# Graph attention scores: destination terms from one matmul, spread by DMA, mask on GpSimd, source term on ScalarE

## What is computed

```python
h = jnp.einsum('blc,oc->blo', x, W).reshape(Bb, Ll, HEADS, HD).transpose(0, 2, 1, 3)   # x is layer-normed, 4 heads of 32
a_src = jnp.sum(h * att_src, axis=-1, keepdims=True)
a_dst = jnp.sum(h * att_dst, axis=-1, keepdims=True)
e = a_src + jnp.swapaxes(a_dst, 2, 3)          # e[i, j] = source score of i + destination score of j
e = jnp.where(e >= 0, e, NEG_SLOPE * e)
e = jnp.where(adj_mask[:, None, :, :], e, fill)
alpha = jax.nn.softmax(e, axis=-1)
out = jnp.einsum('bhij,bhjd->bhid', alpha, h)
```

## Time and profile before

| | |
|---|---|
| median of 3 runs | 1985.65 us (1980.44 to 1990.24) |
| the profiled execution | 1984.17 us, span 1982.4 us |
| PE busy | 1698.9 us, 86% |
| DVE busy | 1450.5 us, 73% |
| ACT busy | 926.4 us, 47% |
| POOL busy | 958.7 us, 48% |
| mean granted TensorE clock | 0.956 |

### The profile page before, as it was taken

One profiled execution on the slowest core, in us unless ns is written; L12 is line 12 of the kernel. 1 busy time (PEld: TensorE's weight loads), 2 busy tenths in 40 slices (PEclk: granted clock), 3 DMA queues, 4 the chain that ended last, 5 costly groups with the idle time before them and its releaser, 6 DMA issues.

```text
span 1982.4 us, 39651 instructions
## 1 busy us (share of the span) xinstructions
PE 1698.9 (86%) x10546; PEld 1308.2 (66%) x10546; DVE 1450.5 (73%) x5051; ACT 926.4 (47%) x2779; POOL 958.7 (48%) x852
## 2 busy tenths in 40 slices
PE   3667777999999999999999999999999999988675
PEld 2545566777777777777777777777777777766343
DVE  3556666878888788788887888888888888865532
ACT  1344433555555554555554555445555555543121
POOL 1143466554445555555544555545555444554433
PEclk9888888999999999999999999999999999988897
DMA  4000111222222212222222222122222222212221
GB/s 121 7 26 20 37 33 37 43 40 41 43 41 43 43 34 37 45 43 42 42 42 41 41 44 43 31 41 44 44 40 43 42 44 40 38 34 40 38 32 18
DMA packets 142416, 79.26 MB, mean 40 GB/s; under 512 B 33048, under 2 KB 137564, under 8 KB 141949
## 3 DMA queue, kind: packets, MB, share of 16 engines
q0 software_dynamic: 47232, 34.92, 12.2%
q1 hardware_dynamic: 94973, 41.80, 8.4%
...
## 4 chain that ended last, share of the span: by engine, by line
PE 54%; DVE 20%; issue 8%; POOL 4%; ACT 4%; DMA 1%; DVEq 0%; POOLq 0%; SPq 0%; ACTq 0%
PE bank L1056 7%; PE bank L1075 6%; PE bank L967 5%; PE bank L1060 5%; PE bank L893 5%; PE bank L1068 4%; PE bank L980 4%; PE bank L1002 3%; PE bank L1009 2%; DVE z L638 2%; PE bank L929 2%; DVE hg L858 2%; POOL routed L398 2%; DVE fx L660 2%; PE bank L1019 1%
## 5 line engine op out<-in xcount | busy, mean ns | idle before, releaser
L419 POOL DMA_INDIRECT out<-ys,xt x264 | 426.3, 1615 | 519.3 <-DMA out<-ys,xt 252.6
L398 POOL DMA_INDIRECT routed<-fx,slot x256 | 256.2, 1001 | 141.5 <-DVE slot L779 77.5
L503 ACT ACTIVATE p<-ub,nm 128x128 f32<-128x128 f32 x512 | 163.6, 390 | 277.4 <-DVE nm L712 277.4
L1075 PE MATMUL bank<-w_s,hsT 128*128 (+1 forms) x1584 | 232.1, 283 | 27.8 <-ACT hsT L545 20.4
L858 DVE SCALAR_TENSOR_TENSOR hg<-sg,bank 128x341 f32<-128x341 f32 x264 | 134.7, 510 | 163.2 <-ACT sg L538 161.8
L1075 PEld LDWEIGHTS bank<-w_s,hsT 128*128 128x128 f32 (+1 forms) x1584 | 205.2, 193 | 68.5 <-issue 61.4
L1056 PE MATMUL bank<-w_s,xT 128*128 x528 | 218.4, 496 | 19.6 <-DVE xT L852 7.7
L1060 PE MATMUL bank<-w_s,xT 128*128 x528 | 202.7, 466 | 4.0 <-DVE hu L866 0.4
L511 ACT ACTIVATE p<-bank,nm 128x128 f32<-128x128 f32 x512 | 145.5, 365 | 118.1 <-DVE nm L718 118.0
L544 ACT ACTIVATE hsT<-bank 128x256 f32<-128x256 f32 x264 | 101.1, 383 | 154.0 <-PE bank L1068 152.8
L1068 PE MATMUL bank<-ident,hu 128*128 128x128 f32 (+1 forms) x792 | 136.3, 282 | 33.1 <-DVE hu L866 15.7
...
## 6 DMA issues: line engine op xcount, KB each, us to landing
xt<-routed SPq DMA_DIRECT2D x264, 65.0 KB, 1.8
xs<-in_x SPq DMA_DIRECT2D x32, 256.0 KB, 3.1
out<-bs SPq DMA_DIRECT2D x32, 256.0 KB, 2.3
out<-ys,xt POOLq DMA_INDIRECT x264, 3.4
routed<-fx,slot POOLq DMA_INDIRECT x256
...
```

What stands on the lines that cost most here:

```text
L398: pool.indirect_dma_start(routed, bass.IndirectOffsetOnAxis(slot[p][:, i:i + 1], 0), fx[i // GB][p][:, i % GB, :], None).then_inc(S[f"sc{p ...
L419: pool.indirect_dma_start(out_rows, bass.IndirectOffsetOnAxis(xt[r][:, C:C + 1].bitcast(I32), 0), ys[r][:], None, compute_op=ALU.add).then ...
L503: last = act.activation(p1[j % 2][:, h, :], ub[j % 2][:, h, :], ACT.Exp, bias=nm1[:, j, h:h + 1])
L1075: last = pe.matmul(y_p[:, 0:C], hsT[r % 2][0:n, c, :], w2_s[0:n, bass.ds(e, 1), c, :].rearrange("p a c -> p (a c)"), start=c == 0, stop=c ...
```

## The change

The destination scores no longer come from `term1`. One matmul (`G.e`) of `wd`, now 128x128 with 4 filled columns, with all of xnT gives all destination scores of the group as 4 rows of 512 numbers. ACT copies them to `dT`. SP writes them to a DRAM buffer `dst_d` (`G.dw`, one DMA) and reads them back with 4 DMAs (`G.dr`), one for each batch, each of which puts the same 512 numbers on all 128 partitions of `dst`. POOL adds the mask in place (`G.m.j`), 512 wide. ACT adds the source score with 4 activations of 128 columns with a bias (`G.a.j`) and writes `ub`. DVE does leaky ReLU in place and the row maximum; its add from PSUM is gone. `mask` and `dst` are double buffered. The table `ORDER` is a new one: not only the new steps but most of the others stand in other places.

```diff
-            wd = sb("wd", [C, NH, L])
+            wd = sb("wd", [C, 128])
...
+                def put_dst():
+                    sp.wait_ge(S["dT"], g + 1)
...
+                    sp.dma_start(dst_d[p * GB:(p + 1) * GB, :].rearrange("b (h l) -> h b l", h=NH), dT[:]).then_inc(S["dd"], 16)
+
+                def get_dst():
+                    sp.wait_ge(S["dd"], 16 * (g + 1))
...
+                    for j in range(GB):
+                        row = dst_d[p * GB + j:p * GB + j + 1, :]
+                        sp.dma_start(dst[p][:, j, :], bass.AP(row.tensor, row.offset, [[0, L], [1, NH * L]])).then_inc(S[f"dq{j}"], 16)
...
+                def cut(j):
+                    pool.wait_ge(S[f"dq{j}"], 16 * (g + 1))
+                    if j == 0:
+                        pool.wait_ge(S["mask"], g + 1)
+                    d = dst[p][:, j, :].rearrange("p (h l) -> p h l", h=NH)
+                    pool.tensor_tensor(d, d, mask[p][:, j, :].unsqueeze(1).broadcast_to([L, NH, L]), ALU.add).then_inc(S["dm"], 1)
...
+                def e():
+                    act.wait_ge(S["dT_ps"], g + 1)
...
+                    act.activation(dT[:].rearrange("h b l -> h (b l)"), g0[0:NH, :], ACT.Copy).then_inc(S["dT"], 1)
+
+                def a_(j):
+                    act.wait_ge(S["dm"], 4 * g + j + 1)
+                    act.wait_ge(S["hE"], 2 * g + 1 + j // 2)
...
+                    for h in range(NH):
+                        o = h * GW + HD
+                        last = act.activation(ub[j % 2][:, h, :], dst[p][:, j, h * L:(h + 1) * L], ACT.Identity,
+                                              bias=hE[:, j, o:o + 1])
+                    last.then_inc(S["u"], 1)
...
                 def scores1(j):
-
-                    dve.wait_ge(S["P_ps"], 4 * g + j + 1)
...
-                    dve.tensor_tensor(tb[:], g0[:].rearrange("p (h l) -> p h l", h=NH),
-                                      hE[:, j, 0:NH * GW].rearrange("p (h w) -> p h w", w=GW)[:, :, HD:HD + 1].broadcast_to([L, NH, L]),
-                                      ALU.add).then_inc(S["t"], 1)
...
+                    dve.wait_ge(S["u"], 4 * g + j + 1)
+                    u = ub[j % 2]
+                    uf = u[:].rearrange("p h l -> p (h l)")
+                    dve.scalar_tensor_tensor(out=uf, in0=uf, scalar=0.2, in1=uf, op0=ALU.mult, op1=ALU.max).then_inc(S["t"], 1)
...
+                def e_():
+                    pe.wait_ge(S["xnT"], g + 1)
...
+                    pe.matmul(g0[:], wd[:], xnT[:].rearrange("c b l -> c (b l)"), start=True, stop=True).then_inc(S["dT_ps"], 1)
...
-                def term1(j):
-
-                    pe.wait_ge(S["mask"], g + 1)
...
-                    pe.matmul(ps[:].rearrange("p (h l) -> p h l", h=NH), identb[:],
-                              mask[:, j, :].unsqueeze(1).broadcast_to([L, NH, L]), start=True, stop=False)
-                    for h in range(NH):
-                        last = pe.matmul(ps[:, h * L:(h + 1) * L], wd[:, h, :], xnT[:, j, :], start=False, stop=h == NH - 1)
```

73 lines of the change are left out of this document (36 added, 37 removed).

## The result

The changed kernel takes 2150.6 us (median of 4 runs, 2137.7 to 2151.5), the kernel before 1985.0 beside it (1980.4 to 1990.2). The ratio is 1.082, 95% interval 1.077 to 1.087: slower by 165.6 us. 2017 was forecast, in a range up to 2055.

A forecast was written before the change was run, and what follows sets the result against it. Taken as bound: POOL's loop, with PE's saving turned into waiting. Slots 27.7 + 0.85 + POOL 24.7 + 2.1 = 55.4 us against 54.2; 26 x 1.2 = +31, start +4, from 1984.2 to 2019, stated as 2017; whole range 1925 to 2055.

The forecast's parts named there:

- the loop from slots through POOL to the next flip: Middle body: slots, POOL's scatters and residual add, M.na, next seam; 55.4 us against 54.2, slower at 0.43.
- POOL's stretch: POOL, from the first row scatter to the end of the last residual add G.v1.3: 16.2 + 8.5 = 24.7 us.
- the scatter's start: POOL starts the first row scatter 0.85 us after DVE has written the slots.
- `M.na` to the flip: Body's end, from DVE's M.na statistics after the last residual add to the next flip of y: 2.1 us.
- the slots are written at 27.7: DVE writes the loop slots 27.7 us after the flip of y, against 33.15 before; bounds 24 and 29.
- the start: Bodies 0 to 5, before the middle bodies: +4 us in sum, between -8 and +15.
- x2 starts at about 7.0: With T.wo just behind the first gate, x2 starts 7.0 us after the flip of y instead of 12.4.
- That is even, so the 20.7 stays: DVE operations leaving and entering the stretch from x2 to the slots' end balance, so it stays 20.7 us.
- The contention: GpSimd and DVE sharing SBUF interfaces: weighed, but the base add's 1252 to 1282 ns showed no stretch.
- Slack in POOL's loop: First rival: POOL's loop has slack, PE's 3.4 us a body comes through; 1900 us in full; 0.30 wholly or in part.
- Late rows: Third rival: destination reads 3 us longer delay u.2 and, through T.ms, the slots; about 2070 us; 0.10 with stretched adds.
- Stretched adds: Third rival's second mechanism: POOL adds beside DVE each 0.3 us longer, four a body; 2050 us; 0.10 with late rows.

The follow-up runs named there:

- e1: Changed kernel with three POOL steps moved: E.s.1 and G.m.3 ahead of the first row scatter, E.s.3 behind the row scatter T.sc.3; 2052.0 us, ratio 1.032.
- e16: Changed kernel plus only two PE matmuls at the seam whose results nobody reads (the fillers); 2110.3 us, ratio 1.062.
- e12: e6 plus two PE matmuls at the seam whose results nobody reads (the fillers); 1988.5 us, ratio 0.999.
- e7: Changed kernel with the four row reads fetching a constant at the body's start, destination scores left out of the result; 2112.8 us, ratio 1.061.
- e14: Changed kernel with constant rows read early, mask adds cut to 4 columns, base add later, expert load E.l.3 ahead of T.f's store; 2072.2 us, ratio 1.043.
- e4: Changed kernel with the four mask adds of a body cut from 512 columns to 4; 2056.5 us, ratio 1.032.
- e5: e1 with SP issuing expert load E.l.3 ahead of T.f's store, which waits for POOL's base add; 2045.0 us, ratio 1.026.
- e6: e5 with POOL's base add moved behind mask add G.m.3, just ahead of the first row scatter; 2048.2 us, ratio 1.028.
- e10: e6 plus two unused PE matmuls at the seam, and mask add G.m.2 moved behind expert scatter E.s.1; 2103.1 us, ratio 1.056.
- e15: e12 with ACT's two copies to kbd issued ahead of its four scaled copies of x2; 2085.2 us, ratio 1.048.

## Why the prediction failed

**What held.** The direction, and the mechanism behind the slots with three of its sizes: the loop from slots through POOL to the next flip bounds the body; POOL's stretch 24.7 (measured 24.80), the scatter's start 0.85 (0.87), `M.na` to the flip 2.1 (2.05). That POOL's 24.8 holds some 2.4 us of waiting for landings is in the sum too, as the 4.0 of two scatters back to back. SP issues the write of dT at 4.83 in the body shown (4.8). DVE waits 3.09 us for POOL before L654 in the body shown, 2.70 in the mean. ACT's waits for the masked rows are small, 14.4 us in all. e1 confirms the loop by shortening it. PE was to be busy 47 of 55; it is busy 675.5/800 x 60 = 51, since its clock is lower. ACT was put at 34 us a body and has 33.9. DVE was to lose 2.8 us with its four adds, and its busy time stays at 44.7 us a body (44.6 before): what left came back as stretched instructions.

**The step that failed** is "the slots are written at 27.7". They are written at 8.74 + 23.56 = 32.30, 4.6 us late, 26 x 4.6 = 120 us. Of the 134 us by which the forecast missed another 16 are the start, 20 us instead of 4, and some 7 the end, put at 0. Against that stands a slip of some 12 us that happened to help: the sum takes 55.4 us less the 54.2 of one quiet body, where the mean body of before, which the prediction has itself, is 54.6. The last step from 2019 to 2017 has no reason either. The step had two terms, and both were wrong.

*"x2 starts at about 7.0".* It starts at 8.74. I wrote that "the clock falls at some seams as it does now; I count that the same on both sides". It does not fall the same on both sides: in us 4 to 8 it is 0.65 against 0.90 before, with 0.9 us more idle time at the seam in front of it. (The prediction put all 3.4 us that PE saves there; most of PE's new idle time stands in the middle of the body.) With the seam filled x2 comes at 7.26 (e16) and 7.07 (e12): the term is the clock, shown. The runs that bring x2 forward without fillers have a higher clock there as well, 0.92 in e7 (x2 at 7.45) and 0.79 in e1 (7.79), and e14 with 0.60 has x2 at 8.88. The page "TensorE: Matmul & The Clock Gate" of the Trainium skill says in Part 1, on the clock gate, that PE's clock has a half rate when idle and the full one when busy; the trace agrees, 2.07 against 1.02 us for one matmul.

*"That is even, so the 20.7 stays".* It became 23.56. I counted instructions that enter and leave the stretch at their lengths of before. The count was even; the lengths were not. DVE is busy 21.5 us of the stretch instead of 18.7, and idle 2.05 us in both. Four entries carry the 2.8: fx 2.25 us instead of 1.18, the copies to kbd 1.68 instead of 0.83, qT 1.16 instead of 0.69, ve_t 0.55 instead of 0.16. POOL's adds stand beside them: the mask adds, the more so because the rows come late (a read 4.1 us, not 2.5), and the base add. Taken away one by one they give 1.4 (e7), 1.56 (e4) and, with the load behind the base add, 0.7 us from e1's value (e5, e6); the three overlap. e14 has 21.35 left, 0.65 above the forecast, and there the copies to kbd, beside the base add, are 1.1 us too long: without that the stretch would be about 20.2, an estimate. By that the 20.7 would have held but for the contention.

**The contention** I had weighed and set aside, since the base add's rows lay within 1252 to 1282 ns "although DVE works beside it all the time". They told of its old neighbours only, and rows 7 don't show what DVE did beside it. In its new place the base add takes 1.81 us, and fx beside it 2.26 instead of 1.23 (e6); one of the copies to kbd takes 1.27 beside a mask add and 0.42 without (e4). The page "SBUF — State Buffer" of the Trainium skill, section "Who interferes with whom", names just these partners: a DVE copy or tensor_scalar in a two-port mode, or a DVE instruction with two SBUF inputs, and a GpSimd instruction that reads SBUF; whichever starts first keeps the port and the other blocks. The trace agrees on the partners: every pair named here is of this kind, and reductions of DVE beside the same adds kept their 0.69 us. In e10 it goes further than one instruction each: the record of the ReLU starts 0.48 us ahead of the first add and ends behind the third. Nor was the leaky ReLU new as an instruction with two SBUF inputs, as I wrote: before the change it read tb twice. The contention should have been a term of the sum, not half of a rival at 0.10.

**The rivals.** Slack in POOL's loop: refuted. Late rows: true in part, 38 us of 166 (e7), by the second of the two ways named, T.ms and the slots, and not through u.2. Stretched adds: true, but the price was put on the wrong side: the base add grows by 0.55 us and a mask add takes 1.39 us in the mean against the 1.26 put for it, while DVE loses 2.8 us a body. What I had as separate rivals all came at once, and with them the clock.

**What stays open.** Why the fillers give 10 us on e1 and 60 on e6: it goes with the clock, which only e12 holds at 1.00 through the whole body, but no run shows that the clock alone does it. What of e15's 3.4 us lies outside the slow matmuls. Whether e14 with the seam filled would have its slots at 27.7; that wasn't run. The contributions do not add up: e1, e4 and e16 give back 99, 94 and 40 us apart, and each raises the clock too. Nor does any run show the path faster than before: in e12 PE has less of the old work, and waits for it. And e12 stands beside a kernel before without fillers, whose own seam has a clock of 0.90 in us 4 to 8; no run gave it the fillers, so the path may still cost what they would bring there.
